# The first twenty microseconds of a gated sequence layer with a routed FFN, set up in another way, and a new order of its steps

## What is computed

```python
ctx = causal_ema(x, tau_ctx)                      # running decayed sum over the positions
wg = sigmoid(concat([x, ctx]) @ Wg.T + bg)        # the gate, two 128x128 halves of Wg
gated = x * wg
h1 = gelu(x @ Wn1.T + bn1)                        # 32 numbers per position
mod = 0.5 + sigmoid(h1 @ Wn2.T + bn2)             # 128 numbers (D) per position
traces = causal_ema(gated * mod[d], tau_d)        # for each of the 128 d
temporal = sum_d traces[d] * softmax(blend)[d]
gate = sigmoid(temporal @ Wtemp.T + btemp)
soma = gelu(x @ Wsoma.T + bsoma)
out = layernorm((soma * gate) @ Wout.T) * gamma + beta
# then: the best half of the positions (by out . w_router) go through a
# 128 -> 512 -> 128 FFN, are weighted, added back, and x is added
```

## Time and profile before

| | us |
|---|---|
| median of 3 runs (175.0 to 176.06) | 175.16 |
| the profiled execution: its own time | 177.31 |
| its span, from first to last instruction | 175.6 |
| TensorE busy in the span | 168.1 (96%) |
| VectorE busy | 134.7 (77%) |
| GpSimd busy | 134.3 (76%) |
| ScalarE busy | 95.5 (54%) |

### The profile page before, as it was taken

How to read it: one execution, slowest core, us unless ns; L and a number is a source line. 1 busy time by engine, 2 the same in 40 slices (tenths; PEclk the granted TensorE clock), 3 DMA queues, 4 the chain that set the end, 5 groups by cost and what they waited for, 6 DMA issues and landing times.

```text
span 175.6 us, 3503 instructions
## 1 busy us (share of the span) xinstructions
PE 168.1 (96%) x1194; PEld 128.7 (73%) x1194; DVE 134.7 (77%) x237; ACT 95.5 (54%) x182; POOL 134.3 (76%) x158
## 2 busy tenths in 40 slices
PE   6499999999999999999999999999999999999993
PEld 5386444876865878966667675888896997887992
DVE  1538996799699876889787899889885787785842
ACT  2429797795662233934117047656924944937450
POOL 7903930597798598899997989999799967896960
PEclk9969999999999999999999999999999999999999
DMA  4997000000000000000000000000001001202123
GB/s 109 261 202 166 16 4 0 0 2 6 0 0 0 4 0 0 0 4 0 0 0 6 0 0 4 0 2 0 6 0 60 4 0 47 74 0 63 60 63 119
DMA packets 12849, 5.62 MB, mean 32 GB/s; under 512 B 2944, under 2 KB 12704, under 8 KB 12832
## 3 DMA queue, kind: packets, MB, share of 16 engines
q1 hardware_dynamic: 11216, 4.68, 10.0%
q10 hardware_dynamic: 1616, 0.72, 1.6%
HBM read 3.30 MB, written 2.10 MB: 31 GB/s over the span
## 4 chain that ended last, share of the span: by engine, by line
PE 90%; DMA 3%; DVE 3%; ACT 1%; SPq 1%; issue 1%
PE ring L1094 28%; PE ring L1160 8%; PE ring L1051 5%; PE ring L1141 4%; PE ring L1109 4%; PE ring L1017 4%; PE ring L1099 4%; PE ring L1065 4%; PE ring L1034 4%; PE ring L1035 3%; DMA down<-in_cond_dram 3%; PE ring L1170 3%; PE ring L1147 2%; PE ring L1042 2%; PE ring L1116 2%; PE ring L1081 2%
## 5 line engine op out<-in xcount | busy, mean ns | idle before, releaser
L495 POOL TENSOR_TENSOR ctx_acc<-ctx_acc,prod 128x192 f32<-128x192 f32 (+18 forms) x75 | 81.3, 1093 | 23.8 <-DVE prod L847 18.8
L847 DVE TENSOR_TENSOR prod<-ring,gm 128x192 f32<-128x192 f32 (+18 forms) x75 | 42.1, 579 | 9.7 <-PE ring L1094 8.0
L1094 PE MATMUL ring<-mod_hi,decayed_lo 128*128 128x512 f32 (+10 forms) x90 | 32.0, 399 | 0.0
L1094 PE MATMUL ring<-mod_lo,decayed_hi 128*128 128x512 f32 (+10 forms) x90 | 26.2, 335 | 0.0
L1094 PE MATMUL ring<-mod_hi,decayed_hi 128*128 128x512 f32 (+10 forms) x90 | 26.2, 334 | 0.0
L1094 PEld LDWEIGHTS ring<-mod_hi,decayed_lo 128*128 128x128 f32 x90 | 15.8, 189 | 7.4 <-issue 5.1
L833 DVE TENSOR_TENSOR state<-ring,blend_w 128x1024 f32<-128x1024 f32 x16 | 18.8, 1219 | 1.0 <-PE ring L1051 0.9
L1094 PEld LDWEIGHTS ring<-mod_lo,decayed_hi 128*128 128x128 f32 x90 | 16.6, 189 | 1.8 <-issue 1.1
L1094 PEld LDWEIGHTS ring<-mod_hi,decayed_hi 128*128 128x128 f32 x90 | 16.5, 188 | 0.9
L1160 PE MATMUL ring<-w_sb,gm 128*128 128x128 f32 x128 | 15.3, 275 | 0.0
L1160 PEld LDWEIGHTS ring<-w_sb,gm 128*128 128x128 f32 x128 | 14.8, 192 | 0.5 <-issue 0.5
(11 more groups left out here) (169 smaller groups left out, 346.8 us busy)
## 6 DMA issues: line engine op xcount, KB each, us to landing
out_dram<-x_nat SPq DMA_DIRECT2D x7, 256.0 KB, 2.3
x_nat<-in_x_dram SPq DMA_DIRECT2D x2, 512.0 KB, 5.9
x_nat<-in_x_dram SPq DMA_DIRECT2D x2, 256.0 KB, 4.4
x_nat<-in_x_dram ACTq DMA_DIRECT2D x1, 512.0 KB, 6.0
w_sb<-in_L_ffn_W_dram SPq DMA_DIRECT2D x2, 256.0 KB, 4.0
out_dram<-x_nat SPq DMA_DIRECT2D x2, 128.0 KB, 1.8
down<-in_cond_dram SPq DMA_DIRECT2D x2, 64.0 KB, 4.6
prod<-in_L_cond_Wg_dram ACTq DMA_DIRECT2D x1, 128.0 KB, 2.9
```

The costliest lines, as they stand in the source:

```text
L495: nc.gpsimd.tensor_tensor(dst, dst, packed(prod[:, n % NP, 0:width(r)], r, k), ALU.add).then_inc(acc_done, 1)
L847: nc.vector.tensor_tensor(dst, packed(slot(step), r, k), lagged(gated(r), r, k), ALU.mult).then_inc(read(step), 1)
L1094: last = nc.tensor.matmul(to[:, c], w[:, k, :], src[:, c], start=(i == 0), stop=(i == len(parts) - 1))
```

## The change

1. `turn_a` no longer has the transpose of `Wn2`; that goes to `turn_c`, which hands the transpose of the falling powers to a new step `turn_g`. `turn_a` now waits for two weight loads and for three short rows.
2. The biases `bn1`, `bg` and `bn2` are loaded as rows of one partition (`vecs`) and turned into columns by three one-column matmuls in `turn_a`. Before they came as columns by six DMAs. VectorE copies `bn1` out with the weights and halves the other two.
3. The third part of `x` (`xt:2`) is loaded on ScalarE's queue behind the second; `Wsoma` moves from there to SP's queue. SP's queue waits for the second part of `x` before it starts the fourth.
4. Two warm-up matmuls follow `turn_a` instead of four.
5. `turn_a` takes one bank of PSUM instead of two.
6. The step `powers` on GpSimd is now called `falling` and stands later.
7. `ORDER` is new throughout. Among other things all four `wg` of the groups 0 to 3 still stand in front, now with no other weights between them, `h1:0` comes before `xt:1`, and `xt:2` before `wg:0`.

```diff
-WARM = (5, 1, 4)
+WARM = (5, 1, 2)
...
-decay:0 xt:0 turn_b:0 decays:0.0 powers:0 context:0 turn_a:0 xt:1 gelu:0 wg:0 soft:0 decays:0.1 context:1
+decay:0 decays:0.0 powers:0 xt:0 turn_b:0 turn_a:0 h1:0 xt:1 context:0 decays:0.1 soft:0 xt:2 context:1
...
-    if kind in ("turn_a", "nat", "out", "up", "scatter"):
+    if kind in ("nat", "out", "up", "scatter"):
...
+        vecs = squares[0:1, 0:3, 0:P]
...
-            sp.dma_start(wn2_in[:, :, :], w_n2[:, None, :].to_broadcast([P, BT, HN])).then_inc(wa_in, 16)
-            sp.dma_start(bias_in[:, 0:1], col(b_g)).then_inc(bias_inn, 16)
-            sp.dma_start(tiles_of(x_nat, 2), tiles_of(x_dram, 2)).then_inc(x_in[2], 16)
-            sp.dma_start(bias_in[:, 1:2], col(b_n2)).then_inc(bias_inn, 16)
-            for g in range(BT):
-                sp.dma_start(bn1[g * HN:(g + 1) * HN, :], col(b_n1)).then_inc(bn1_in, 16)
+            sp.dma_start(vecs[:, 0, :].rearrange("o (g h) -> o g h", g=BT),
+                         b_n1.rearrange("(o g h) -> o g h", o=1, g=1).to_broadcast([1, BT, HN])).then_inc(rows_in, 16)
+            sp.dma_start(vecs[:, 1, :], b_g.rearrange("(o n) -> o n", o=1)).then_inc(rows_in, 16)
+            sp.dma_start(vecs[:, 2, :], b_n2.rearrange("(o n) -> o n", o=1)).then_inc(rows_in, 16)
+            sp.dma_start(wn2_in[:, :, :], w_n2[:, None, :].to_broadcast([P, BT, HN])).then_inc(wn2_done, 16)
+
+            sp.wait_ge(x_in[1], 16)
             for r in range(3, R):
                 sp.dma_start(tiles_of(x_nat, r), tiles_of(x_dram, r)).then_inc(x_in[r], 16)
...
+            sp.dma_start(wsoma_in, w_soma).then_inc(ws_in, 16)
...
-            act.dma_start(tiles_of(x_nat, 1), tiles_of(x_dram, 1)).then_inc(x_in[1], 16)
-            act.dma_start(wsoma_in, w_soma).then_inc(ws_in, 16)
+            for r in range(1, 3):
+                act.dma_start(tiles_of(x_nat, r), tiles_of(x_dram, r)).then_inc(x_in[r], 16)
...
                 if kind == "turn_a":
-                    nc.vector.tensor_copy(turned_w[:, :], slot(step)[:, 0:2 * P + HN]).then_inc(read(step), 1)
-                    nc.vector.tensor_copy(wn2_t[:, :], slot(step)[:, BANK:BANK + P]).then_inc(read(step), 1)
+                    n = 2 * P + HN + 1
+                    nc.vector.tensor_copy(turned_w[:, :], slot(step)[:, 0:n]).then_inc(read(step), 1)
+                    nc.vector.tensor_scalar(bias_h[:, 0:2], slot(step)[:, n:n + 2], 0.5, None, ALU.mult).then_inc(
+                        read(step), 1)
...
                 if kind == "turn_a":
-                    pe.wait_ge(wa_in, 3 * 16)
-                    pe.wait_ge(ident_done, 1)
+                    pe.wait_ge(wa_in, 2 * 16)
+                    pe.wait_ge(rows_in, 3 * 16)
+                    pe.wait_ge(ident_done, 2)
...
-                    last = nc.tensor.transpose(dst[:, BANK:BANK + P],
-                                               wn2_in[:, :, :].rearrange("p g h -> p (g h)"), ident[:, :])
+                    for i in range(3):
+                        at = 2 * P + HN + i
+                        last = nc.tensor.matmul(dst[:, at:at + 1], vecs[:, i, :], ones[0:1, 0:1], start=True, stop=True)
...
                 elif kind == "turn_c":
                     pe.wait_ge(soft_done, 1)
+                    pe.wait_ge(wn2_done, 16)
+                    nc.tensor.transpose(dst[:, 0:P], sexp, ident[:, :])
+                    last = nc.tensor.transpose(dst[:, P:2 * P], wn2_in[:, :, :].rearrange("p g h -> p (g h)"),
+                                               ident[:, :])
+                elif kind == "turn_g":
                     pe.wait_ge(falling_done, 1)
```

More of the change, by code:

```diff
@@ new lines @@
+turn_c:0 wg:0 xt:3 context:2 wg:1 context:3 gated:0 gated:1 table:0.0 table:0.1 table:0.2 wg:2 gated:2 mod:0
+table:0.3 falling:0 split:0 wg:3 h1:1 low:0 turn_g:0 early:0 gated:3 unit:0.0 unit:0.12 unit:0.6 unit:0.2
+mod:1 h1:3 split:1 unit:0.11 unit:0.3 turn_f:0 low:1 mod:3 unit:0.1 unit:0.5 h1:2 nat:0.0 unit:0.15 unit:1.0
+unit:1.5 unit:0.13 unit:1.10 mod:2 unit:0.9 unit:1.3 unit:1.15 state:0.0 unit:0.4 early:1 soma:1 unit:1.9
+nat:1.0 nat:1.1 early:2 unit:0.7 rw:0 rising:0 unit:0.14 unit:1.6 unit:1.2 unit:1.11 plus_beta:0 state:1.0
@@ L723, in _ @@
                 kind, r, k = step
-                if kind in ("turn_a", "turn_b", "turn_c", "turn_d", "turn_e", "turn_f", "nat", "state", "unit",
+                if kind in ("turn_a", "turn_b", "turn_c", "turn_d", "turn_e", "turn_f", "turn_g", "nat", "state", "unit",
                             "down", "scatter"):
```

88 lines of the change are left out of this document (43 added, 45 removed).

## The result

The changed kernel takes **183.24 us** (median of 6 runs, 182.32 to 184.99), the kernel before 175.59 (6 runs, 175.0 to 176.89) on the same chip: a ratio of **1.0432, 95% interval 1.0368 to 1.0496**. It is slower by some 7.6 us. (Single executions of one kernel spread over some 2 us, and each ratio here leaves out those that lie over 1.5% above the fastest of their kernel.) The forecast was 173.7 within 171.8 to 176.6, faster or the same in 86 of 100 cases. It is wrong in sign and outside its range.

The account below looks back on a forecast made before the run. TensorE, busy 96% of the span, was taken as the bound behind a front; -1.7 in the front and +0.2 behind it gave -1.5, so 175.16 became 173.7 us, range 171.8 to 176.6.

Parts of the forecast that it names:

- When `turn_a` can begin: Start of `turn_a`, waiting for weights and rows: 6.9 instead of 8.2, so -1.3 us (-2.0 to +1.0).
- `turn_a` itself: Length of `turn_a`: one transpose fewer, three one-column matmuls more, 0.3 us each, overlapped: +0.2 us (0 to +0.5).
- From there to `xt:1`: Between `turn_a` and `xt:1`: two warm-up matmuls hidden by `h1:0`'s wait, 1.2 us for 1.34: -0.1.
- Losing two warm-up matmuls: Warm-up before `xt:1`: no cost unless the clock suffers; `xt:1` left at 1.72 us (bound: -0.9).
- the lost clock is not in the timed runs: Rival, front: timed runs before lack the low clock, so the front wins only about 0.9: 174.4 us, chance 0.13.
- The front in sum: Everything up to `wg:1`: it starts 1.7 us earlier, 15.4 for 17.07 (between 3.0 earlier and 0.6 later).
- Behind the front: After `wg:1` starts: same matmuls, only waits can be lost: +0.2 us (-0.7 to +4).
- VectorE becomes the bound: Rival, after the first unit: VectorE over about 95% busy, TensorE waits at later steps: +2.3, 177.5 us, chance 0.12.
- two signs of being wrong: `turn_a` starting after 8.2, or TensorE's waits on VectorE or GpSimd behind 16 us adding to more than 1.

Follow-up runs that it names:

- a_small_first: Changed kernel with the `bg` and `bn2` row loads moved to ScalarE's queue behind `Wg`, ahead of the second part of `x`: 180.08 us, ratio 1.027.
- m_oldorder: Changed kernel with the order of the kernel before, `falling:0` put behind `table:0.3` and `turn_g:0` behind `h1:1`: 179.43 us, ratio 1.020.
- a_both: `a_small_first` with the order of `a_gp2`: 182.07 us, ratio 1.035.
- a_warm12: Changed kernel with twelve warm-up matmuls ahead of `turn_a` instead of one: 182.39 us, ratio 1.040.
- a_res_early: `a_gp2` with `residual:1` moved up on GpSimd to directly behind `var:2`, ahead of `unit:4.12` and `unit:4.6`: 178.71 us, ratio 1.0125.
- a_gp2: Changed kernel with `plus_beta:2` moved behind `residual:1` and `stats:2.1` moved up to behind `normed:1`: 183.56 us, ratio 1.043.
- a_beta_late: Changed kernel with `plus_beta:2` moved on GpSimd from before `unit:4.14` to behind `residual:1`: 181.89 us, ratio 1.032.

## Why the prediction was wrong

**"When `turn_a` can begin ... I take 6.9": mis-sized.** It was 8.56 in the changed kernel's profile, and 7.0 to 7.4 in five others with the same loads, so the range (6.2 to 9.2) held it and the choice within it was too early, by 0.1 to 1.7. `Wn1` was taken as nearest in kind; it landed after 2.6 here. (The last row was the sixth issue of the queue, at 3.50, not the fifth at 3.3.) What separates an early from a late small load was in the trace of before and was read as something else: the second part of `x` was issued at 2.23; `Wn1`, issued at 1.86, landed after 4.3, and `Wn2` and the bias column, issued at 2.33 and 2.79, after 5.8 and 5.9. The rows' descriptors were not what decided (`a_small_first` has the same). The prediction called 9.2 the likelier end by a rule and didn't follow it; no profile reached 9.2, one came within 0.7 and five lie nearer to the 6.9. The rule that a semaphore lands only behind earlier writes of its DMA engine on all queues stands in the Trainium skill under DMA: Bandwidth & Descriptors, "Queues, rings and completion order", and rows that are late behind `x` fit it, though no trace shows a row's landing. The confinement of the four copies to few engines isn't borne out as the cause: that row, issued at 2.32 in `a_small_first`, held nothing.

**"`turn_a` itself ... +0.2": mis-sized, +0.65.** Three one-column matmuls of float32 are six records; they took 0.64 in `m_oldorder`, 0.94 here, where the clock falls among them, and 1.23 at the low level (`a_both`). The row gave 0.3 for the two records of one such matmul, and "overlapped" was an assumption: at the high level three of them add to 0.64, and 0.3 more is the clock.

**"From there to `xt:1` ... -0.1": +0.4**, for the same reason, since it ran at the low level and `h1:0` was reckoned at 0.43 where it took 0.59.

**"Losing two warm-up matmuls costs nothing unless the clock suffers ... (bound: -0.9)": the bound had the wrong side.** Only a gain was allowed for. The low stretch now takes in `xt:2` as well, which before ran at the high level (with `xt:3`, 1.91 for both). `a_warm12` shows its price in this front (`wg:1` 1.3 earlier though `turn_a` was 0.7 later), and with `turn_a` at 5.7 a low level throughout costs 2.4 us (`a_both` against `a_small_first`). That two warm-up matmuls fewer caused it isn't shown; in `a_res_early`, with the same two, the low stretch lasts 3.4 us (8.79 to 12.21) as before. The rival "the lost clock is not in the timed runs" had the mechanism right, a clock whose course differs between executions of the same front, and asked only about the kernel before.

The front in sum: forecast -1.7 (its terms as written add to -1.6), measured +1.6 in the changed kernel's profile and -0.5 to -0.95 in four other profiles of the same front. With the rows ahead of `x` it was -2.9 (`a_small_first`), about the forecast's best of -3.0. So the front fell short of its forecast, and the size of this varies with the execution.

**"Behind the front. Every step's matmuls are the same ones. What can be lost is a wait. ... I put +0.2 (... to +4)": this is the step that failed**, +4.5. The sentence is right, and the look that followed stopped at the first unit. It followed VectorE through 14 to 31 us and found it safe, which it was. No step was taken to the place where three engines, one `o_sb` half and a ring of banks meet, though the order tells of it without any time: `out:3.0` two words behind `residual:1` where it had stood 13 behind, `up:1.1` nine further and in the banks of `out:3.0`. When `residual:1` would run could be read from the trace before: it starts 117.3 behind `wg:1`, and still does.

**The rival "VectorE becomes the bound" was the right sign by the wrong mechanism.** VectorE had 14.50 of 20 in the stretch with the loss. It was neither engine's amount of work but the place of a few words: with the same work, `residual:1` moved up by seven words on top of `a_gp2`'s moves, the loss of 4.5 became 0.2 (`a_res_early`). And its price of 4 left the clock out: a stand-still of 3.1 cost another 1.7.

Of the prediction's two signs of being wrong, the first came (`turn_a` at 8.56, after 8.2). The second, TensorE's waits on VectorE or GpSimd of over 1 us, was worded past the fault: the 3.1 us are a wait on ScalarE, which waits for GpSimd. And VectorE, which was to be watched, had 7.62 of 10 from 27 to 37 us.

## What to carry to other kernels

When engines run a hand-written order, look in the new order for each pair of a reader of a buffer and the writer that must wait for it, and measure how far apart they are now, in whose queue the reader stands, and whose banks the next matmuls take. Totals of busy time say nothing of it, and thinning the reader's queue doesn't mend the wait if what is ahead of it is itself waiting (`a_beta_late`, `a_gp2`). Issue every small load that the first compute step needs before any queue starts a large one. And an order carried over to another bank placement may meet new waits (`m_oldorder`). For a repair, try first a step that uses no banks: here moving `residual:1` helped, and moving `up` gave all later steps other banks and made it worse. Compare a variant by all its executions before calling it better.
